# Adjacency columns by pieces with two under way, and the residual product moved beside the units of a sparse graph attention layer on one Trainium2 core

## What is computed

```python
h = relu(layernorm(x))
hh = (h @ W.T).reshape(n, 8, 32)
s_src, s_dst = sum(hh * a_src, -1), sum(hh * a_dst, -1)
attn = s_src[:, None] + s_dst[None] + adj[:, :, None] * We + be
attn = softmax(leaky_relu(where(adj > 0, attn, -inf), 0.2), axis=1)
out = x + (attn @ hh) + h @ Wr.T + br
```

## Time and profile before

| what | us |
|---|---|
| median of three executions | 2688.48 |
| profiled execution | 2684.95 |
| its span on the core, first to last instruction | 2683.3 |
| DVE busy | 2132.3 (79%) |
| POOL busy | 1485.7 (55%) |
| ACT busy | 1246.5 (46%) |
| PE busy | 1235.0 (46%) |

### The profile page before, as it was taken

How to read it: one execution, slowest core, us unless ns; L and a number is a source line. 1 busy time by engine, 2 the same in 40 slices (tenths; PEclk the granted TensorE clock), 3 DMA queues, 4 the chain that set the end, 5 groups by cost and what they waited for, 6 DMA issues and landing times.

```text
span 2683.3 us, 27007 instructions
## 1 busy us (share of the span) xinstructions
PE 1235.0 (46%) x5305; PEld 934.2 (35%) x5306; DVE 2132.3 (79%) x4852; ACT 1246.5 (46%) x4898; POOL 1485.7 (55%) x1666
## 2 busy tenths in 40 slices
PE   6990022503334367446424524533341453518885
PEld 4660022402324245334322512422241342416664
DVE  3448959998998898999889988988997841259992
ACT  2320030221245498667546546444542655826662
POOL 5772656756675777777777476277347437710000
PEclk9995556757666676666666666666665666759998
DMA  3665656686676877877777677678668614477660
GB/s 114 195 228 191 216 131 195 167 249 178 179 226 192 225 240 225 245 229 243 229 224 239 199 233 222 183 231 233 208 193 234 200 39 100 95 225 173 157 156 3
DMA packets 226527, 512.79 MB, mean 191 GB/s; under 512 B 98280, under 2 KB 116400, under 8 KB 224208
## 3 DMA queue, kind: packets, MB, share of 16 engines
q1 hardware_dynamic: 151280, 319.60, 37.2%
q0 software_dynamic: 74960, 191.61, 28.1%
q10 hardware_dynamic: 144, 0.13, 0.0%
HBM read 475.19 MB, written 36.03 MB: 191 GB/s over the span
## 4 chain that ended last, share of the span: by engine, by line
DMA 56%; issue 18%; PE 10%; DVE 6%; POOL 6%; ACT 2%; SPq 1%; POOLq 0%; DVEq 0%; ACTq 0%; PEldq 0%
DMA adj_sb<-in_adj_dram 40%; DMA arena<-table,arena 8%; DMA arena<-table,own 6%; POOL arena L493 5%; PE banks L1058 2%; PE banks L1052 2%; ACT arena L947 1%; PE banks L1101 1%; DVE work L619 1%; PE banks L1079 1%; DVE work L615 1%; PE banks L1055 1%; PE banks L1154 1%; PE banks L1144 1%; DMA out_dram<-w_all,arena 1%
## 5 line engine op out<-in xcount | busy, mean ns | idle before, releaser
L493 POOL DMA_INDIRECT arena<-table,arena x943 | 972.6, 1031 | 354.5 <-issue 231.2
L1079 PE MATMUL banks<-arena,ident 128*128 128x256 f32 x1268 | 426.9, 513 | 1142.1 <-DVE arena L755 1142.1
L947 ACT ACTIVATE arena<-arena,prob 128x32 f32<-128x32 f32 x4024 | 859.5, 306 | 2.1
L1079 PEld LDWEIGHTS banks<-arena,ident 128*128 128x128 f32 x1268 | 332.6, 268 | 1234.8 <-issue 984.6
L615 DVE MAX8 work<-adj_sb 128x8 f32<-128x184 f32 (+51 forms) x624 | 580.9, 1005 | 116.0 <-DMA adj_sb<-in_adj_dram 115.5
L619 DVE FIND_INDEX8 work<-work,adj_sb 128x8 uint32<-128x184 f32 (+51 forms) x624 | 618.6, 1013 | 0.0
L942 ACT ACTIVATE prob<-pre 128x104 f32<-128x104 f32 (+26 forms) x63 | 20.3, 322 | 965.6 <-DVE pre L739 965.6
L1085 PE MATMUL banks<-arena,ident 128*128 128x256 f32 x1006 | 312.6, 442 | 106.3 <-ACT arena L947 106.2
L493 POOL DMA_INDIRECT arena<-table,own x194 | 202.2, 1042 | 157.4 <-DMA arena<-table,own 55.6
L1085 PEld LDWEIGHTS banks<-arena,ident 128*128 128x128 f32 x1006 | 197.3, 212 | 209.0 <-ACT arena L947 188.5
L932 ACT ACTIVATE pre<-arena,we_all 128x13 f32<-128x13 f32 (+23 forms) x480 | 146.5, 400 | 80.1 <-DMA arena<-lists 80.1
(11 more groups left out here) (140 smaller groups left out, 1789.2 us busy)
## 6 DMA issues: line engine op xcount, KB each, us to landing
adj_sb<-in_adj_dram SPq DMA_DIRECT2D x504, 512.0 KB, 4.0
arena<-dst_rows SPq DMA_DIRECT2D x16, 2048.0 KB, 8.5
arena<-table,arena POOLq DMA_INDIRECT x943, 3.5
table<-arena POOLq DMA_DIRECT2D x32, 264.0 KB, 2.9
arena<-in_x_dram SPq DMA_DIRECT2D x32, 256.0 KB, 3.0
resid<-arena POOLq DMA_DIRECT2D x32, 256.0 KB, 2.6
out_dram<-arena POOLq DMA_DIRECT2D x32, 256.0 KB, 2.8
work<-table SPq DMA_DIRECT2D x8, 1024.0 KB, 10.9
```

What stands on the lines that cost most here:

```text
L493: pool.indirect_dma_start(gath[:, un.slot(k), :], None, table[:, :], bass.IndirectOffsetOnAxis(ap=rec[:, k, 0:1], axis=0), bounds_check=N ...
L947: last = s.activation(g, g, ACT.Copy, scale=prob[:, b, k * H + h:k * H + h + 1])
L1079: last = m.matmul(ps_sum[:, u % 2, :], ident[:, :], gath[:, un.slot(k), 0:HD], start=(k == 0), stop=False)
```

## The change

Four things are changed.

1. The first stage makes neither the residual nor the turned scores. It writes the relu output, turned, to an internal array `normed`, and keeps the destination scores of all tiles in SBUF. The scores are turned by four transposes after the stage, and written by four transfers from ACT.
2. The residual is made by tile: ACT issues two loads (`normed` and x), PE makes four products (two for Wr, one that adds br, one that adds x through the identity), ACT copies the result and issues two stores. 13 tiles are made before the first unit and then one per unit, behind the unit's sums on PE and behind its weighting on ACT.
3. The adjacency pieces of all tiles go with two under way, each on a semaphore of its own; a piece is issued as soon as the segments of tile c-2 that lie in its columns are searched. DVE starts a segment's MAX8 when its pieces have landed, and does each segment's FIND_INDEX8 one MAX8 later, with a semaphore increment on each.
4. The ring has 81 slots instead of 86. A group's first store waits until the residual rows of its tiles have landed.

```diff
-GSLOTS = 86
+GSLOTS = 81
+RES_FIRST = 13
...
             for c, so in enumerate(sources):
                 b = c % 2
-                if c >= 2:
-                    sp.wait_ge(S["scanned"], c - 1)
                 for n in range(PIECES):
                     cols = slice(n * PIECE, (n + 1) * PIECE)
-                    if n and so.t >= 16:
-                        sp.wait_ge(S[f"adj_in{b}"], 16 * (c // 2 * PIECES + n))
-                    sp.dma_start(adj_sb[:, b, cols], load_adj(so.t)[:, cols]).then_inc(S[f"adj_in{b}"], 16)
+                    lane = S[f"adj_in{b}{n % 2}"]
+                    if c >= 2:
+                        sp.wait_ge(S["scanned"], segs_before[c - 2] + scans_of(sources[c - 2], n))
+                    if n >= 2:
+                        sp.wait_ge(lane, 16 * (c // 2 * (PIECES // 2) + n // 2))
+                    sp.dma_start(adj_sb[:, b, cols], load_adj(so.t)[:, cols]).then_inc(lane, 16)
...
-                    pool.wait_ge(S["dst_copied"], u + 1)
-                    pool.dma_start(dst_rows[:, bass.ts(u, 2 * P)].rearrange("h (b p) -> h b p", b=2),
-                                   dst_sb[0:H, q, :, :]).then_inc(S[f"dst_out{q}"], 16)
-                    pool.wait_ge(S["res_done"], u + 1)
-                    nc.gpsimd.tensor_tensor(rt_sb[:, q, :, :], rt_sb[:, q, :, :],
-                                            br_all[:, :].unsqueeze(1).to_broadcast([P, 2, HD]), ALU.add
-                                            ).then_inc(S["br_added"], 1)
-                    pool.wait_ge(S["br_added"], u + 1)
-                    pool.dma_start(by_unit(resid, u), rt_sb[:, q, :, :]).then_inc(S[f"res_out{q}"], 16)
-                    pool.dma_start(by_unit(out, u), rt_sb[:, q, :, :]).then_inc(S[f"res_out{q}"], 16)
+            def keep_normed(u, q):
+
+                pool.wait_ge(S["hnT_done"], u + 1)
+                pool.dma_start(normed[bass.ts(u, 1), :, :].rearrange("a p n -> (a p) n"),
+                               hnT[:, q, :, :].rearrange("p b n -> p (b n)")).then_inc(S[f"normed_out{q}"], 16)
...
             def store(un):
 
                 pool.wait_ge(S["evac"], un.u + 1)
+                if un.place in (None, 0):
+                    rows = un.group.t0 + un.group.n if un.group else un.source.t + 1
+                    for b in range(3):
+                        if rows > b:
+                            pool.wait_ge(S[f"res_out{b}"], 32 * ((rows - b + 2) // 3))
...
             def add_biases(u, q):
 
                 dve.wait_ge(S["hd_copied"], u + 1)
+                v.tensor_copy(sd_all[:, bass.ts(u, 2), :], hd_sb[:, q % 2, :, HD:ROW])
                 v.tensor_tensor(s_all[:, bass.ts(u, 2), :], hd_sb[:, q % 2, :, ROW:ROW + H],
                                 be_all[:, :].unsqueeze(1).to_broadcast([P, 2, H]), ALU.add).then_inc(S["s_done"], 1)
...
-                v.tensor_tensor(rt_sb[:, q % 2, :, :], ps_res[:, q % 2, :, :], x_sb[:, q, :, :], ALU.add
-                                ).then_inc(S["res_done"], 1)
...
-                for s in range(so.segs):
-                    last = v.max(val8[:, 8 * s:8 * s + 8], a[:, bounds[s]:bounds[s + 1]])
-                last.then_inc(S["maxed"], 1)
-                dve.wait_ge(S["maxed"], c + 1)
-                for s in range(so.segs):
-                    last = v.max_index(idx8[:, 8 * s:8 * s + 8], val8[:, 8 * s:8 * s + 8],
-                                       a[:, bounds[s]:bounds[s + 1]])
-                last.then_inc(S["scanned"], 1)
+
+                def index(s):
+
+                    dve.wait_ge(S["maxed"], segs_before[c] + s + 1)
+                    v.max_index(idx8[:, 8 * s:8 * s + 8], val8[:, 8 * s:8 * s + 8],
+                                a[:, bounds[s]:bounds[s + 1]]).then_inc(S["scanned"], 1)
+
+                for s in range(so.segs):
+                    pieces = -(-bounds[s + 1] // PIECE)
+                    for lane in range(2):
+                        if pieces > lane:
+                            dve.wait_ge(S[f"adj_in{b}{lane}"], 16 * (c // 2 * (PIECES // 2) + (pieces - lane + 1) // 2))
+                    v.max(val8[:, 8 * s:8 * s + 8], a[:, bounds[s]:bounds[s + 1]]).then_inc(S["maxed"], 1)
+                    if s:
+                        index(s - 1)
+                index(so.segs - 1)
...
+            def load_residual(t):
+
+                b = t % 3
+                if t >= 3:
+                    act.wait_ge(S[f"res_out{b}"], 32 * (t // 3))
+                act.dma_start(hx_sb[b][:, 0:IN], normed[t // 2, :, t % 2 * IN:(t % 2 + 1) * IN]).then_inc(S[f"hx_in{b}"], 16)
+                act.dma_start(hx_sb[b][:, IN:2 * IN], x[bass.ts(t, P), :]).then_inc(S[f"hx_in{b}"], 16)
+
+            def residual(t):
+
+                b = t % 3
+                act.wait_ge(S["res_ps"], t + 1)
+                s.activation(hx_sb[b][:, IN:2 * IN], ps_res[:, t % 2, :], ACT.Copy).then_inc(S["res_done"], 1)
+                act.wait_ge(S["res_done"], t + 1)
+                act.dma_start(out[bass.ts(t, P), :], hx_sb[b][:, IN:2 * IN]).then_inc(S[f"res_out{b}"], 16)
+                act.dma_start(resid[bass.ts(t, P), :], hx_sb[b][:, IN:2 * IN]).then_inc(S[f"res_out{b}"], 16)
+                if t + 2 < TILES:
+                    load_residual(t + 2)
...
+            for t in range(RES_FIRST):
+                residual(t)
             prepare(units[0])
             for un in units:
                 if un.u + 1 < len(units):
                     prepare(units[un.u + 1])
                 exps(un)
+                if un.u and RES_FIRST + un.u - 1 < TILES:
+                    residual(RES_FIRST + un.u - 1)
...
                     for c in range(2):
-                        rows = hnT[:, q, b, c * P:(c + 1) * P]
-                        m.matmul(ps_hd[:, q, b, :], rows, w_all[:, c, 0:272], start=(c == 0), stop=(c == 1))
-                    for c in range(2):
-                        rows = hnT[:, q, b, c * P:(c + 1) * P]
-                        m.matmul(ps_dst[0:H, q, b, :], w_all[:, c, HD:ROW], rows, start=(c == 0), stop=(c == 1))
-                    for c in range(2):
-                        rows = hnT[:, q, b, c * P:(c + 1) * P]
-                        last = m.matmul(ps_res[:, q, b, :], rows, w_all[:, c, 272:528], start=(c == 0), stop=(c == 1))
+                        rows = hnT[:, q4, b, c * P:(c + 1) * P]
+                        last = m.matmul(ps_hd[:, q, b, :], rows, w_all[:, c, 0:272], start=(c == 0), stop=(c == 1))
...
                 tile_sums(un)
+                if RES_FIRST + un.u < TILES:
+                    residual(RES_FIRST + un.u)
                 for group in groups:
                     if group.ranked_at == un.u and not group.at_once:
                         ranks(group)
```

More of the change, by code:

```diff
@@ L357, in listed, with scans_of @@
                 landed(eng, un.group.load_seq + 1)
+        segs_before = [sum(so.segs for so in sources[:c]) for c in range(len(sources))]
+        def scans_of(so, n):
+            return sum(lo < (n + 1) * PIECE for lo in segments(so.segs, so.power)[:-1])
         load_adj = lambda t: adj[bass.ts(t, P), :]
@@ L473, in _ @@
+            for q in range(4):
+                pool.wait_ge(S[f"normed_out{q}"], 16 * (UNITS // 4))
             pool.wait_ge(S["pad_out"], 16)
@@ L519, in load_dealt @@
                 landed(pool, group.deal_seq + group.n)
+                if group.g == 0:
+                    pool.wait_ge(S["dst_out"], 64)
                 if group.g >= 2:
@@ L1104, in ranks @@
                          ).then_inc(S["rank_ps"], 1)
+            pe.wait_ge(S["s_done"], UNITS)
+            for q in range(4):
+                last = m.transpose(ps_dst[:, q * P:(q + 1) * P],
+                                   sd_all[:, q * 16:(q + 1) * 16, :].rearrange("p t h -> p (t h)"), ident[:, :])
+            last.then_inc(S["dst_ps"], 1)
+            for t in range(RES_FIRST):
+                residual(t)
             for un in units:
```

103 lines of the change are left out of this document (67 added, 36 removed).

## The result

| | before | after |
|---|---|---|
| median, us | 2687.43 | 2609.02 |
| lowest and highest | 2681.77 to 2694.1 | 2606.22 to 2612.89 |
| span of the profiled execution | 2683.3 | 2604.3 |

The change makes the kernel faster: 0.9708 of the time before, 95% interval 0.9681 to 0.9736. That is 78 us, half of the forecast 155, and 9 us outside the range.

What follows compares the result with a forecast made beforehand. PE was taken to bound the first stage, then DVE's searches with late gathers and adjacency waits, POOL up to 1217 us. Terms -66 - 12 + 14 - 96 + 5 = -155 gave 2533 us, range 2480 to 2600.

Steps and rivals of the forecast that it cites:

- First stage, -66: First stage: without residual product and turned scores a step falls from 5.46 to 3.45 us, DVE's chain next; -66 us.
- The rival of the clock: First stage: PE's clock may fall to 1.2 GHz, gaining 7 to 15 us instead of 66; 2592 us, chance 0.07.
- To unit 3, -12: First search to unit 3: two late-gather holes of 47.2 us shrink by 12, net of the residual's traffic.
- Units 3 to 17, +14: POOL-bound stretch up to unit 17: 8 us from slower gather transfers plus ACT's 6; bounds -5 and +50.
- The 6 us of ACT: Units 7 to 17: the residual's work on ACT loses 6 us, counted within the +14.
- POOL a little late: Rival: gathers go at 1.60 instead of 1.43 us; +45 - 8 in the POOL-bound stretch, 2582 us, chance 0.11.
- Units 17 to 52, -91: Unit 17 to the last ranks: adjacency waits of 106.5 us go whole, less residual costs on ACT and at last ranks.
- the 4 us of overlap in the search: Late searches: FIND_INDEX8 no longer held by the MAX8 before it, 0.12 us for each of 33 tiles; 4 us gained.
- The end, 0: After unit 62, dense tile and what follows: no change forecast, 0 us.
- neither is touched: The gather-limited tail and the dense tile: the change was said to touch neither, so no term was given.
- pieces share: Rival: two pieces under way land twice as late; half the wait stays, +48, 2581 us; all, 2629; chance 0.07.
- POOL the bound: Rival: gathers 0.45 us slower each make POOL the limit, 2807 us; decides from about 0.3 us more; chance 0.04.

Runs made afterwards that it cites:

- e3: The kernel before with only the adjacency pieces two under way, early release and paired search; residual stays in the first stage: 2591.03 us, 0.9606 of the kernel before.
- e4: The kernel after with adjacency pieces and search as before, so the residual moved without the pieces' change: 2742.45 us, 1.0158 of the kernel before.
- e2: The kernel after with 32 increments of an unused semaphore at the head of ACT's program, moving its flag loop: 2558.03 us.
- e1: The kernel after with 64 increments of an unused semaphore at the head of ACT's program: 2563.85 us, 0.9515 of the kernel before.
- e5: The kernel before with 82 semaphore increments at ACT's head, its flag loop 64 past a multiple of 128 instructions: 1.019 of the kernel before.
- e9: The kernel after with 32 semaphore increments at ACT's head, timed again on another chip: 2697.36 us, 0.946 of the kernel before by the medians.

## Why the prediction was half right

**First stage, -66: right.** Measured -66.7. A step was put at 3.45 us, on DVE's chain. In the kernel after the statistics of three successive steps start at these times:

```profile
100.29 0.75 DVE L586 BATCH_NORM_STATS2 arena<-arena 128x6 f32<-128x256 f32 x2 [0.38 <-DVE s_all L606]
...
103.61 0.75 DVE L586 BATCH_NORM_STATS2 arena<-arena 128x6 f32<-128x256 f32 x2 [0.38 <-DMA arena<-in_x_dram]
...
107.32 0.75 DVE L586 BATCH_NORM_STATS2 arena<-arena 128x6 f32<-128x256 f32 x2 [0.73 <-DVE s_all L606]
```

3.32 and 3.71 us; over 26 steps from 40 us on the mean is 3.52. That the total is met to 0.7 us is in part luck: the steps give 62 us of it and the start and the drain the rest. PE is busy 64.9 of 90 us, at a granted clock of 0.98 (the 2.4 GHz level), with a gap ahead of each step's transposes, 1.02 us before the one at 102.80. The rival of the clock is out.

**To unit 3, -12: wrong by 11.** The two holes were to shrink from 47.2 us by 12. They stayed:

```profile
302.34 0.78 DVE L757 TENSOR_TENSOR pre<-pre,arena 128x600 f32<-128x600 f32 x1 [26.28 <-DMA arena<-table,own]
...
608.17 0.65 DVE L757 TENSOR_TENSOR pre<-pre,arena 128x392 f32<-128x392 f32 x2 [18.31 <-DMA arena<-table,arena]
```

26.3 + 18.3 = 44.6 us. e3 and e4 split it: the pieces alone gained 8.7 us, the residual alone lost 15.1, and beside the pieces it lost 465.6 - 458.0 = 7.6. The step that failed is the netting at "I take 12": the residual's 6.8 MB took the pieces' gain back almost whole.

**Units 3 to 17, +14: a size too small.** POOL sets the end of the stretch, as forecast, but its chain grew by 23.5 us where 8 was put down: 0.09 us for each of the 266 transfers instead of 0.03. This term was mis-sized. Half of it comes from the pieces (12.2 in e3), half from the residual (10.2 in e4). The 6 us of ACT weren't a cost on top: DVE waited 5.5 us for ACT in units 6 to 17, but for rows 37.0 us, the longest time at unit 15, where the earlier trace rows had 5.07:

```profile
1115.14 0.40 DVE L757 TENSOR_TENSOR pre<-pre,arena 128x232 f32<-128x232 f32 x1 [18.60 <-DMA arena<-table,arena]
```

This is the rival "POOL a little late" at under half of its price: 15.5 us above the forecast where it had 45 - 8 = 37.

**Units 17 to 52, -91: nearly right, -85.** The wait of 106.5 us went whole. Two under way gave 4.9 us from issue to landing in the whole run, 2.4 us a piece, where 2.6 was taken:

```profile
adj_sb<-in_adj_dram SPq DMA_DIRECT2D x504, 512.0 KB, 4.9
```

In units 17 to 50 DVE waits 2.3 us for ACT's exponentials in e3, without the residual, and 15.4 in the kernel after. So the residual costs 13 us there, and the forecast had 11.6. But not where it was put. In the kernel after, the sums behind the exponentials of units 24 and 32:

```profile
1375.37 0.39 DVE L772 TENSOR_REDUCE rsum<-prob 128x8 f32<-128x136 f32 x1 [2.93 <-ACT prob L975]
...
1581.35 0.36 DVE L772 TENSOR_REDUCE rsum<-prob 128x8 f32<-128x120 f32 x1 [3.54 <-ACT prob L975]
```

The wait falls in the unit behind each group's first, since the residual stands behind the first unit's long work on ACT and ahead of the next one's exponential. DVE's busy time fell from 845.7 to 841.1, the 4 us of overlap in the search. The Trainium skill, "VectorE: DVE Perf Modes", section "The DRAIN you can't avoid", read in full, doesn't speak against these 4 us: the same paragraph says that a next operation which isn't held starts earlier. The trace agrees: in the kernel after a FIND_INDEX8 starts with its load at 1240.29, 0.08 us before the MAX8 ahead of it ends (1239.36 + 1.01). Left are rows that came 10.9 us late at unit 23, which the 3 us for local lateness didn't hold, and 5.4 us of ACT that waited before too. From unit 17 to unit 23 POOL waited for its own lanes and never for DVE, so its delay reached this unit; e3 has the same wait, 11.2 us, so the residual isn't behind it. The last ranks didn't come later (8.6 us after, 9.6 before), where 5 had been put down. The sum: -106.5 + (22.3 - 5.4) + 10.9 + (8.6 - 9.6) - 4.5 = -84.2.

**Tail, 0: right. The end, 0: wrong by 50.** This is the step that failed: "neither is touched" put the end at nothing. It was true of every instruction there and false of the place of ACT's code. The prediction didn't ask why the trace of before had 25 us after its last computing instruction, nor what moves when ACT's program gets 338 instructions longer. What the runs showed in its place is ACT's walk over the flags at 8.3 us a flag instead of 1.3, with 38 code fetches. With this mended the kernel takes 2558 (e2, one execution) to 2564 us (e1), inside the range; against the 2696 of the kernel before on that chip it gains 132 to 138 of the forecast 155 us.

Of the rivals, "pieces share" didn't come: two under way landed after 4.9 us against 4.0 in the whole run, not after twice as long. "POOL the bound" didn't come either, but POOL is close to being the limit: it set the pace up to unit 23, and from unit 17 to 50 it waited for DVE's ranks only 22.5 us, where the earlier trace rows had 95.2 + 78.5 of waits for DVE. Two sums beside the forecast are slightly off and change nothing in it: with steps of 4.9 to 5.2 us the clock's rival gains 8 to 18 us in the first stage, not 7 to 15, and what the range leaves out adds up to about 0.11 (0.04, 0.03 and half of 0.07), not 0.15.

## What to carry to other kernels

A part of a kernel that no edit touches can still change if code ahead of it grows: look for a tail in which no engine computes, and for instruction fetches in it, and try a few idle instructions ahead of a long loop before judging an edit (here some 45 us, more than half of what the change showed). Where loads go one after the other and the consumer waits for them, a second one in flight removes the wait even at a longer latency each, and it also makes room for traffic moved beside it. Price moved traffic by the queue that has no slack: here that was POOL's, where the residual made each transfer 0.04 us later and the pieces 0.05.

## What the runs showed of the hardware

- A loop of 254 instructions on ACT, of which a pass runs a few and jumps over the rest, took 1.3 us a pass, and 8.3 us when it lay elsewhere, with 38 fetches of 8 KB of code in the 72 us that hold its last seven passes, in three kernels (after, e4, e5). The same loop on DVE took 1.5 us in all of them.
- PE kept a granted clock of 0.98 with 72% of its time busy and a gap of about 1 us in every step of 3.5; in the dense tile 219.6 busy of 304 us went with 0.86.
- The same kernel (32 increments) took 2558 us on one chip and 2608 to 2707 on another. There ACT's weightings (one head of a slot each) came every 1.4 us for a stretch, as in the first two lines, of e9; the kernel after, last line, does 112 of them in 23.84 us. The cause is open:

```profile
1027.06 0.32 ACT L982 ACTIVATE arena<-arena,prob 128x32 f32<-128x32 f32 x1 [1.08 <-issue]
1028.46 0.32 ACT L982 ACTIVATE arena<-arena,prob 128x32 f32<-128x32 f32 x1 [1.08 <-issue]
...
877.65 23.84 ACT L980 ACTIVATE arena<-arena,prob 128x32 f32<-128x32 f32 x112
```
